# Steps without tiles reordered in a vision-transformer layer: the next step's mixing, features and moments put elsewhere, and half of w2 loaded in the setup

## What is computed

```python
pooled = x.reshape(64, 12, 14, 16, 14, 16).sum(axis=(3, 5))      # x: 64 images of 12 x 224 x 224
h = einsum('bcij,ce->bije', pooled, channel_weights)             # 196 tokens of 192 per image
q, k, v = heads(layernorm(h) @ w_qkv)                            # 12 heads of 16
a = relu(1 + qk + qk**2 / 2);  a = a / a.sum(-1)                 # attention by a polynomial
h = h + (a @ v) @ w_proj + b_proj
g = layernorm(h);  top_w, top_i = top_k(softmax(g @ router.T), 2)
for e in range(8):                                               # two of eight experts for each token
    out = out + w_e * (gelu(g @ w1[e] + b1[e]) @ w2[e] + b2[e])
return h + out
```

## Time and profile before

| | us |
|---|---|
| median of 3 runs | 1280.63 (1279.28 to 1282.81) |
| the profiled execution | 1280.55 |
| its span in the trace | 1278.7 |
| from the features of step 1 to those of step 2, and of step 2 to step 3 | 40.00 and 40.37 |
| from the features of step 3 to its mask | 32.5 |

### The profile page before, as it was taken

How to read it: one execution, slowest core, us unless ns; L and a number is a source line. 1 busy time by engine, 2 the same in 40 slices (tenths; PEclk the granted TensorE clock), 3 DMA queues, 4 the chain that set the end, 5 groups by cost and what they waited for, 6 DMA issues and landing times.

```text
span 1278.7 us, 25861 instructions
## 1 busy us (share of the span) xinstructions
PE 1195.3 (93%) x7219; PEld 1073.0 (84%) x7219; DVE 883.1 (69%) x2860; ACT 598.6 (47%) x1143; POOL 557.9 (44%) x453
## 2 busy tenths in 40 slices
PE   5868766999999999999999999999999999999996
PEld 3766655989888898989888888898989899999996
DVE  6788888787878787969697878787845223223443
ACT  0222224454645454546454645454555445454564
POOL 0104433325454545463636363636373753443533
PEclk9986566999999999999999999999999999999998
DMA  9788988778888888797979797979453854454555
GB/s 352 243 294 332 334 311 280 248 233 253 248 257 251 259 238 272 231 277 224 283 215 295 211 295 213 293 214 293 107 134 79 252 117 108 91 105 97 105 138 117
DMA packets 124823, 284.41 MB, mean 222 GB/s; under 512 B 23091, under 2 KB 68772, under 8 KB 124772
## 3 DMA queue, kind: packets, MB, share of 16 engines
q1 hardware_dynamic: 82570, 241.95, 56.4%
q0 software_dynamic: 41568, 41.24, 18.5%
q10 hardware_dynamic: 634, 0.61, 0.2%
HBM read 228.79 MB, written 54.95 MB: 222 GB/s over the span
## 4 chain that ended last, share of the span: by engine, by line
PE 73%; DVE 15%; issue 5%; ACT 3%; DMA 2%; SPq 1%; POOL 0%; ACTq 0%; DVEq 0%; POOLq 0%
PE ps L1003 25%; PE ps L972 21%; PE ps L812 6%; PE ps L919 4%; PE ps L943 3%; PE ps L944 3%; PE ps L908 3%; PE ps L898 2%; DVE red L1084 2%; PE ps L886 2%; DVE red L1081 1%; DVE topi L1220 1%; PE ps L876 1%; PE ps L1001 1%; DMA w1r<-L_attn_w_qkv 1%
## 5 line engine op out<-in xcount | busy, mean ns | idle before, releaser
L629 POOL DMA_INDIRECT result<-ys,ridx x210 | 331.7, 1580 | 305.1 <-ACT ys L770 164.4
L1003 PE MATMUL ps<-w2a,hid 128*128 x2520 | 457.5, 327 | 0.0
L1003 PEld LDWEIGHTS ps<-w2a,hid 128*128 128x128 f32 x2520 | 416.1, 190 | 11.7 <-issue 0.2
L614 POOL DMA_INDIRECT rows_d<-rows,sloti x224 | 217.7, 972 | 363.3 <-ACT rows L726 299.9
L737 ACT ACTIVATE hid<-ps,b1s 128x512 f32<-128x512 f32 (+1 forms) x344 | 222.9, 654 | 233.3 <-PE ps L972 222.9
L1084 DVE TENSOR_REDUCE red<-xbuf 128x21 f32<-128x672 f32 x344 | 279.0, 842 | 4.8 <-PE ps L876 2.4
L972 PE MATMUL ps<-xh,w1h 128*128 128x512 f32 (+1 forms) x344 | 163.6, 476 | 7.2 <-DVE xb L1329 7.1
L1340 DVE TENSOR_TENSOR w1l<-w1r,w1h 128x768 fp32r<-128x768 f32 x116 | 110.5, 953 | 81.1 <-ACT w1h L749 80.4
L972 PE MATMUL ps<-xb,w1h 128*128 128x512 f32 (+1 forms) x344 | 130.1, 378 | 0.0
L972 PE MATMUL ps<-xh,w1l 128*128 128x512 f32 (+1 forms) x344 | 130.1, 378 | 0.0
L972 PE MATMUL ps<-xl,w1h 128*128 128x512 f32 (+1 forms) x344 | 129.9, 378 | 0.0
(11 more groups left out here) (162 smaller groups left out, 1557.9 us busy)
## 6 DMA issues: line engine op xcount, KB each, us to landing
xbuf<-x SPq DMA_DIRECT2D x224, 672.0 KB, 6.2
w1r<-L_ffn_w SPq DMA_DIRECT2D x118, 384.0 KB, 4.8
xr<-rows_d SPq DMA_DIRECT2D x48, 402.0 KB, 3.9
result<-h1s SPq DMA_DIRECT2D x16, 588.0 KB, 7.4
w2a<-L_ffn_w SPq DMA_DIRECT2D x8, 576.0 KB, 7.0
rows_d<-pad SPq DMA_DIRECT2D x9, 402.0 KB, 4.4
rows_d<-rows,sloti POOLq DMA_INDIRECT x224
result<-ys,ridx POOLq DMA_INDIRECT x210
```

What stands on the lines that cost most here:

```text
L614: pool.indirect_dma_start(rows_d, bass.IndirectOffsetOnAxis(ap=sloti[:, k * RT + t:k * RT + t + 1], axis=0), rows[:, t, :], None).then_inc ...
L629: pool.indirect_dma_start(out, bass.IndirectOffsetOnAxis(ap=ridx[:, b, n:n + 1], axis=0), ys[:, b, n, :], None, compute_op=ALU.add).then_i ...
L1003: last = mm(yout(g, b, n), hid[:, m % 3, cols], w, start=False, stop=m == MC - 1 and n % 2 == 1)
```

## The change

The lists `STEP_ALONE` and `LAST` are rewritten, with new names. `T1` (next mixing) stands ahead of `S8` and writes bank 7 of PSUM instead of bank 1, so that it no longer waits for ACT's second residual copy. `T2` stays behind `S10`. `T3` and `T4` are `S3` and `S4` of the next step (banks 3 to 5 for `S3`), done at the end of a step: `T3` behind `R` and ahead of `V.0`, `T4` between `V.1` and `V.2`. `S9` moves ahead of `V.1` but stands behind `T3`. The sums `P` have other places. Four of the eight pieces of `w2` load in the setup, behind 21 chunks of `x` and ahead of the padding; the others in steps 0 and 1, two each.

```diff
-STEP_ALONE = """S3 P P P P P P P P P P P P P P P P S4 S5 P P S6.0 S6.1 P S6.2 P S6.3 S7.0 P P S7.1 P P S8.0 P S8.1 P S8.2 P P S8.3
-    T1 S10 T2 R V.0 V.1 S11 V.2 V.3 S9 Q0 Q1 Q2 Q3""".split()
+STEP_ALONE = """P P P P P P P P P P P P P P P P S5 P P S6.0 S6.1 P P S6.2 S6.3 S7.0 P P S7.1 P P P P P P T1 S8.0 S8.1 S8.2 S8.3 S10 T2
+    R T3 V.0 S11 S9 V.1 T4 V.2 V.3 Q0 Q1 Q2 Q3""".split()
-LAST = """S3 P P P P P P P P P P S4 S5 P P P G0 G4 S6.0 S6.1 S6.2 S6.3 S7.0 P S7.1 P P G5 G1 P S8.0 S8.1 S8.2 S8.3 S10
-    R V.0 S11 V.1 V.2 S9 V.3 Q0 Q1 Q2 Q3 P P P G2 P P P P G3 P P P P""".split()
+LAST = """S5 P P P P G0 G4 P P S6.0 S6.1 P P S6.2 S6.3 S7.0 P P S7.1 P P G5 G1 S8.0 P P S8.1 P P S8.2 P P S8.3 S10
+    R V.0 S11 V.1 V.2 S9 V.3 Q0 Q1 Q2 Q3 P P G2 P P P P G3 P P P P""".split()
+W2_FIRST = NE - 4
...
+            def load_w2(e0, n):
+                for e in range(e0, e0 + n):
+                    sp.dma_start(w2a[:, e].rearrange("p m f -> p (m f)"), w2[e]).then_inc(d_w2, 16)
+
+            load_w2(0, W2_FIRST)
             set_wait(sp, "pool", "pad")
...
-                if isinstance(s, int) and s < PRO - 1:
-                    for e in range(s * NE // (PRO - 1), (s + 1) * NE // (PRO - 1)):
-                        sp.dma_start(w2a[:, e].rearrange("p m f -> p (m f)"), w2[e]).then_inc(d_w2, 16)
+                if isinstance(s, int) and s < 2:
+                    load_w2(W2_FIRST + 2 * s, 2)
...
             def T1(s):
-                pe.wait_ge(s_h1, s * 4 + 2)
-                S1(s + 1)
+                S1(s + 1, 7)
+
+            def T3(s):
+                S3(s + 1, 3)
+
+            def T4(s):
+                S4(s + 1)
```

More of the change, by code:

```diff
@@ L458, in after_first @@
             return not isinstance(s, int) or s > 0
-        def later(stage):
-            return lambda s, *a: stage(s, *a) if after_first(s) else None
         def wait_first(eng, signal, value):
@@ L683, in _, with S3 @@
             given("act", "qk", copy(qk[:].rearrange("p a h u -> p (a h u)"), ps[0:HD, 5, 0:2 * HEADS * U]))
-            def S3(s):
+            def S3(s, first=0):
                 act.wait_ge(s_g, s + 1)
-                copy(gts[:].rearrange("p i f -> p (i f)"), ps[0:U, 0, 0:IPS * NF]).then_inc(s_gts, 1)
+                copy(gts[:].rearrange("p i f -> p (i f)"), ps[0:U, first, 0:IPS * NF]).then_inc(s_gts, 1)
                 act.wait_ge(s_phT, s + 1)
-                copy(phiT[:].rearrange("p (a b) -> p a b", a=2), ps[0:NF, 1:3, 0:IPS * TOK]).then_inc(s_phTs, 1)
+                copy(phiT[:].rearrange("p (a b) -> p a b", a=2),
+                     ps[0:NF, first + 1:first + 3, 0:IPS * TOK]).then_inc(s_phTs, 1)
             def S4(s):
@@ L798, in _ @@
                     S4(0)
-            schedule(act, {"S3": later(S3), "S4": later(S4), "S5": S5, "S7": S7, "S8": S8, "V": V, "M": M, "W": W,
+            schedule(act, {"S3": S3, "S4": S4, "T3": lambda s: S3(s + 1, 3), "T4": lambda s: S4(s + 1), "S5": S5, "S7": S7, "S8": S8, "V": V, "M": M, "W": W,
                            "X": X, "Y": Y, "G1": G1, "G2": G2, "G3": G3})
@@ L868, in _, with S1 @@
             given("pe", "amat", last)
-            def S1(s):
+            def S1(s, bank=1):
                 pe.wait_ge(s_pooled, s * PARTS + PARTS)
@@ L875, in S1, with S3 @@
                         o = g * NTOK + hf * TOK
-                        last = mm(ps[0:TOK, 1, hf * 96:(hf + 1) * 96], red[:, o:o + TOK], mixg[:, g],
+                        last = mm(ps[0:TOK, bank, hf * 96:(hf + 1) * 96], red[:, o:o + TOK], mixg[:, g],
                                   start=g == 0, stop=g == GROUPS - 1)
                 last.then_inc(s_mix, 1)
-            def S3(s):
+            def S3(s, first=0):
                 pe.wait_ge(s_phi, s + 1)
@@ L885, in S3 @@
                         t = 2 * i + hf
-                        last = mm(ps[0:U, 0, i * NF:(i + 1) * NF], phi[:, t, 0:U], phi[:, t, :],
+                        last = mm(ps[0:U, first, i * NF:(i + 1) * NF], phi[:, t, 0:U], phi[:, t, :],
                                   start=hf == 0, stop=hf == 1)
@@ L889, in S3 @@
                 for t in range(NT):
-                    last = turn(ps[0:NF, 1 + t // IPS, (t % IPS) * TOK:(t % IPS + 1) * TOK], phi[:, t, :])
+                    last = turn(ps[0:NF, first + 1 + t // IPS, (t % IPS) * TOK:(t % IPS + 1) * TOK], phi[:, t, :])
                 last.then_inc(s_phT, 1)
@@ L1043, in T1 @@
             def T1(s):
-                pe.wait_ge(s_h1, s * 4 + 2)
-                S1(s + 1)
-            schedule(pe, {"S1": S1, "T1": T1, "S3": later(S3), "S4": later(S4), "S5": S5, "S6": S6, "S7": S7, "S8": S8,
+                S1(s + 1, 7)
[3 more added lines that the diff above has]
+                S4(s + 1)
+            schedule(pe, {"S1": S1, "T1": T1, "S3": S3, "T3": T3, "S4": S4, "T4": T4, "S5": S5, "S6": S6, "S7": S7, "S8": S8,
                           "S9": S9, "M": M, "X": X, "N": N, "G2": G2, "G3": G3})
@@ L1162, in _, with S2 @@
             att_ch = att[:, :, E:E + C]
-            def S2(s, round=None, both=False):
+            def S2(s, round=None, bank=1, both=False):
                 if round is None:
@@ L1168, in S2 @@
                 dve.wait_ge(s_mix, s + 1)
-                mixed = ps[0:TOK, 1, 0:192].rearrange("p (a b c) -> p a b c", a=2, b=2 * IPS)
+                mixed = ps[0:TOK, bank, 0:192].rearrange("p (a b c) -> p a b c", a=2, b=2 * IPS)
                 att4 = att_ch.rearrange("p (b a) c -> p a b c", a=2)
@@ L1192, in T2 @@
                 before = pos_["step"]
-                S2(s + 1, s, both=True)
+                S2(s + 1, s, 7, both=True)
                 ahead.append(pos_["step"] - before)
```

## The result

The changed kernel takes **1305.99 us** (median of 6 runs, 1302.95 to 1309.07) against 1280.21 of the kernel before beside it: a ratio of 1.0198 [1.0184, 1.0212]. It is 25.8 us slower; the forecast was 33.6 slower, 1314. The profiled execution took 1305.45, its span 1303.6 (before 1278.7).

The account below looks back on a forecast made before the run. A ring of waits among engines in the steps without tiles was taken to bound the first 220 us. 7.6 + 10.9 + 10.5 + 4.6 = 33.6 us for steps 0 to 3 on 1280.55 gave 1314 us, range 1297 to 1322.

Parts of the forecast that it names:

- The ring: Chain of waits in the steps without tiles, from F (PE starting a step's features) to next F, 40.00 us before.
- The tanh: ACT's tanh, queued behind turned-feature copies, runs at F+5.2, not F+0.13; DVE's sums begin at F+7.1 instead of F+2.24.
- The barrier of all sums ahead of the residual: PE begins mixing only after all 14 sums, ending at F+31.3, and stands some 4 us; residual starts behind mixing.
- the residual at the low clock: PE's 14 residual products at 1.2 GHz, behind the mixing: 9.4 us instead of 4.8, ending at F+42.4.
- step 1: Second step without tiles: next F at F+50.9 against 40.00, +10.9 us.
- step 0: First step without tiles: four sums instead of two after the last division, then mixing and slow residual, +7.6 us.
- rival (a): Residual runs at the high clock, 4.8 us instead of 9.4: 1298 us; chance 0.15, whole or for the greater part.
- Step 3: Last step without tiles (LAST, no mixing): sums begin late, mask ready at F+37.1 against 32.54, +4.6 us.
- `w2` at nothing: Half of w2 loaded in the setup costs and gains nothing; SP's load at 47.13 goes to about 54.
- (b): Chunks come late: with the longest landing, 2.8 us late in three steps, 1322 us; chance 0.05.
- (c): Transfers bind the steps, so w2 pieces leaving them are worth 6.6 us: faster, 1274 us; chance 0.04.
- (d): Sums are off the ring, DVE finishing its 14 by F+22.8: 1280 us, no change; chance 0.04.

Follow-up runs that it names:

- e1: Kernel after with V.0 (tanh and first normalised rows) moved ahead of T3, ranking S9 still behind T3: 1302.95 us, ratio 1.0185.
- e2: Kernel after with V.0 (tanh), S11 (gates) and S9 (ranking) all ahead of T3: 1299.14 us, ratio 1.0148.
- e3: Kernel after with T1 (next mixing) back behind the residual S8, all sums still ahead of S8: 1289.05 us, ratio 1.0069.
- e7: Kernel after with 14 idle products on PE ahead of the mixing's wait in steps 0 to 2: 1303.52 us, ratio 1.0170.
- e4: Kernel after with tanh, gates and ranking ahead of T3 and the mixing behind the residual: 1280.60 us, ratio 1.0001.
- e5: Kernel before with only the changed LAST list of step 3: 1286.29 us, ratio 1.0044.
- e8: Kernel after with tanh, gates and ranking ahead of T3, mixing behind the residual, and LAST's sums where they were before: 1278.25 us, ratio 0.9975.
- e6: Kernel before with only half of w2 loaded in the setup: 1280.62 us, ratio 0.9996.

## Where the prediction was right, and where wrong

**The ring and the direction: right.** The end followed the steps without tiles: 24.05 us are lost before the loop, 0.8 behind it.

**The tanh: right, shown by e1 and e2.** First gate after 4.75 us of waiting (forecast about 4.6), first sum at F+6.99 (7.1), first division at F+20.13 (20.3), last sum done at F+31.1 (31.3). The statement beside it, that the ranking behind `T3` isn't later than this, held too: DVE did not wait for it. But the tanh only hid it. Once the tanh is early, the ranking alone holds DVE for 3.27 us (e1), which didn't matter for the sum and does for whoever repairs only the tanh.

**The barrier of all sums ahead of the residual: right, shown by e3.** PE stood 4.18 us ahead of the mixing (forecast some 4).

**The term that was mis-sized: the residual at the low clock.** The forecast took 1.5 us for the mixing and 9.4 for the residual, and chose the low level because PE waits and stands in the new order. The kernel after, cut behind the clock's rise in step 1 (columns as in the earlier trace rows):

```profile
92.70:133.50 40.80, 24.31 (x113) 20.38 (x114) 31.03 (x66) 8.12 (x17) 13.14 (x14) 0.50 0.65 247
133.60:140.30 6.70, 4.09 (x24) 3.77 (x23) 4.09 (x35) 1.80 (x4) 0.00 (x0) 1.00 0.98 376
```

The clock stayed at 1.2 GHz through the stand and the mixing, but went to 2.4 at 133.56, 1.6 us into the residual. So the mixing took 2.1 from its start to the residual's (0.6 more than forecast; the upper end named was 2.5) and the residual 5.7, 3.7 less. Together that is 3.1 us a step: 10.9 − 3.1 = 7.8 for step 1 (measured 7.79), 10.5 − 3.1 = 7.4 for step 2 (7.31), 7.6 − 3.1 = 4.5 for step 0 (4.55). The whole difference in these steps is these two terms, and they hang on the one choice of the clock. The reason given for 1.5, that most of the mixing is issue and the last product's way through, was wrong: the same stretch took 1.1 at the high level in e7 (129.35 to 130.46), so nearly all of it grows with the clock. That all three steps come out alike is in part luck: in e1's step 1 the rise came 2.6 us later behind the start of the mixing, and that step was 1.6 us longer than e1's step 2. The prediction had said that it would be wrong if the residual took under 6 us, and so it was, in this term; rival (a), with its 4.8, was nearer for the residual, though not for the mixing. Neither end was met because the clock changes inside the residual; the forecast named that case, with 1308 to 1318, and gave it too little.

The Trainium skill ("TensorE: Matmul & The Clock Gate", "Part 1: The HAM clock gate") says that sustained activity lifts the throttle. By this rule alone the residual had to become fast soon, and it did: the rise came 3.7 us behind the mixing's start. The forecast preferred, where it came 13 us into a run. A row of the old order, with other work around it, was too little to set against the rule. Why the rise came so late in that row, no run here shows.

**Step 3: right in size, wrong in its reason.** Its walk gave the first division at F+15.4 (measured 15.69) and the mask done at F+37.1 (36.49; its start is at F+36.28). DVE of the kernel after there (F is 194.13):

```profile
201.12 3.00 DVE L1088 TENSOR_REDUCE red<-xbuf 128x42 f32<-128x1344 f32 x2
...
209.82 0.31 DVE L1209 RECIPROCAL rden<-ps 98x24 f32<-98x24 f32 x1 [0.48 <-PE ps L921]
...
222.99 0.36 DVE L1218 BATCH_NORM_STATS2 stats<-h1s 112x6 f32<-112x192 f32 x1 [0.41 <-ACT h1s L717]
```

But the text set out from the sums' late begin, and that is worth nothing: with early sums the mask is at F+35.64 to 35.79 (e2, e4, e5), with late ones at F+35.78 and 35.74 (e3, e7). Of the 4.0 us 3.4 come from four sums that moved behind the numerators (e8 puts them back). The other half microsecond, in the kernel after and in e1, goes with a wait for the residual (0.41 at 222.99), which e3 does not have: the last product of the residual starts at F+29.8 in the kernel after, where eight products of it ran at the low clock, and at F+29.1 in e3. The walk had the four sums in it; what was missing was the question of which of its entries made the difference.

**`w2` at nothing: right, shown by e6.** SP's load went from 47.13 to 53.04 alone and 52.42 in the kernel after, for about 54.

**Rivals.** (b), late chunks, and (c), transfers that bind, did not happen: sums had no idle time ahead of them (page of the kernel after), and the steps that lost a `w2` piece were not shorter for it (e6).

```profile
L1088 DVE TENSOR_REDUCE red<-xbuf 128x42 f32<-128x1344 f32 x52 | 77.4, 1541 | 0.0
```

(d), sums off the ring, asked for a DVE that finishes them by F+22.8, and did not happen either: the last one ended at F+31.1. Nearest to it is e4, with the tanh in front and the mixing behind: its gathered sums end at F+27.1, and behind them DVE still waits for parts of the residual.

What stays open: which part of the rest makes e8's steps shorter, the earlier `T3` and `T4` or the gathered sums, wasn't separated, nor why 2.9 us and not 5 reach the median.

## What to carry to other kernels

Where engines work through lists in strict order, look up for each name that moves what stands behind it on every engine: a small activation put behind a copy, a ranking put behind a transposition and a product put behind a barrier each held an engine that had work to do. Undoing one of two such moves may bring little (e1) because the other holds the same work; undo both before judging either. And spread work that fills gaps by where the gaps are: in step 3 four sums that moved from ahead of a wait to behind it cost 3.4 of their 5.8 us.

## What the runs showed of the hardware

When TensorE's clock rises was the surprise. In step 1 of the kernel before it rose 13 us into work with hardly a break. In steps 1 and 2 of the kernel after it rose 3.7 us behind the start of the mixing, with a stand of 4.18 and 4.17 us just ahead of it; in the same steps of e1 and e2, with the same stand, between 3.2 and 6.3 us behind it. In e7, with idle products in place of the stand, it rose at 127.4 in step 1, 2.4 us after these began, and 4.2 us after they began in step 2. So a stand just ahead did not keep the clock low, but its rise had no fixed place in the work either.

What it costs here is small: each of the fourteen products of the residual takes 0.67 us at 1.2 GHz and 0.34 at 2.4, and PE is on the path only for part of a step. But it blurs the steps. Steps 0 to 2 of e5 follow the list of the kernel before, and were 0.9 and 0.5 us longer and 1.3 shorter; step 0 of e1 has the order of the kernel after up to F of step 1, and was 1.0 longer. So a difference of a microsecond between a step in one trace and the same step in another says nothing by itself.
